# A four-layer graph network on one core: three extra TensorE products behind each lot of four pairs in both plain edge sums

## The reference

```python
# layer 0 (GIN)
agg = jax.ops.segment_sum(x[src], dst, num_segments=N)
h = (1.0 + eps) * x + agg
h = _prelu(_bn(h @ W1 + b1, gamma1, beta1), a1)
h = _prelu(_bn(h @ W2 + b2, gamma2, beta2), a2)
...
# layers 1 and 2: graph attention (two rounds) and a relational attention layer with an FFN
...
# layer 3 (GCN): x @ W, each edge's row scaled by the degrees of its two ends, summed at the destination,
# then bias, relu, the residual and a layer norm
```

## Time and profile before the change

| | value |
|---|---|
| median of 3 runs | 9297.23 us (9285.59 to 9308.83) |
| profiled execution, from first to last instruction (its span) | 9269.7 us; the page gives no other time of that execution |
| mean granted TensorE clock | 0.703 of 2.4 GHz |
| gin_sum, from the first lot's products to the last's | 150 to 1200 us |
| gcn_sum, the same | 8095 to 9231 us |
| busy shares of the span | POOL 60%, DVE 55%, PE 51%, ACT 21% |

### The profile page before, as it was taken

How to read it: one execution, slowest core, us unless ns; L and a number is a source line. 1 busy time by engine, 2 the same in 40 slices (tenths; PEclk the granted TensorE clock), 3 DMA queues, 4 the chain that set the end, 5 groups by cost and what they waited for, 6 DMA issues and landing times. The chain is left out here.

```text
span 9269.7 us, 86837 instructions
## 1 busy us (share of the span) xinstructions
PE 4716.6 (51%) x20222; PEld 3105.8 (34%) x20222; DVE 5109.9 (55%) x19512; ACT 1943.8 (21%) x4901; POOL 5545.9 (60%) x5485
## 2 busy tenths in 40 slices
PE   2232342444433444479677777777765555523223
PEld 1222232333422333434233333333324555423122
DVE  3233362444443444586677777777778888624234
ACT  0000021222211222220122222222224444400001
POOL 6767616666636666511566666666646666467674
PEclk6555565555565555589899889989877778756566
DMA  2111112222222222258777777777757777111111
GB/s 65 48 46 47 44 37 62 69 69 69 68 52 62 71 70 71 54 221 318 246 229 236 230 226 232 235 228 234 228 159 211 212 212 212 59 46 46 46 48 44
DMA packets 466182, 1195.68 MB, mean 129 GB/s; under 512 B 107396, under 2 KB 145252, under 8 KB 452504
## 3 DMA queue, kind: packets, MB, share of 16 engines
q0 software_dynamic: 275744, 782.99, 30.5%
q1 hardware_dynamic: 175468, 382.51, 12.4%
q10 hardware_dynamic: 14476, 24.62, 0.8%
HBM read 1004.41 MB, written 185.28 MB: 128 GB/s over the span
## 5 line engine op out<-in xcount | busy, mean ns | idle before, releaser
L943 POOL DMA_INDIRECT gat_ring<-gat_table,psrc_idx x1664 | 1652.6, 993 | 1080.0 <-issue 479.9
L579 DVE TENSOR_TENSOR acc<-acc,bank 128x129 f32 (+1 forms) x1664 | 480.0, 288 | 1461.7 <-remote 1156.1
L1936 POOL DMA_INDIRECT pair<-right_table,idx_r_idx x782 | 783.1, 1001 | 656.4 <-PE bank L1990 215.3
L1138 DVE TENSOR_TENSOR acc<-acc,bank 128x130 f32 x1664 | 482.3, 290 | 1178.7 <-remote 898.7
L511 POOL DMA_INDIRECT gcn_sum_ring<-gcn_table,src_idx x782 | 791.2, 1012 | 358.6 <-issue 231.9
L511 POOL DMA_INDIRECT gin_sum_ring<-in_x,src_idx x782 | 773.1, 989 | 359.3 <-issue 229.3
L1936 POOL DMA_INDIRECT acc<-left_table,idx_l_idx x782 | 809.0, 1035 | 290.3 <-issue 202.0
L1007 PE MATMUL bank<-gat_ring,gat_hot 128*128 128x130 f32 x3328 | 760.7, 403 | 423.9 <-DVE gat_hot L1127 234.6
L2012 ACT ACTIVATE positive<-positive 128x512 f32<-128x512 f32 x782 | 492.8, 630 | 1956.3 <-DVE positive L2042 1265.2
L2101 POOL DMA_INDIRECT x_rows<-left_table,idx_l_idx x586 | 609.3, 1040 | 440.8 <-DVE weighted L2214 229.1
L1990 PE MATMUL bank<-pair,ident 128*128 128x512 f32 x1564 | 871.2, 641 | 0.0
(11 more groups left out here) (522 smaller groups left out, 8184.1 us busy)
## 6 DMA issues: line engine op xcount, KB each, us to landing
gat_place<-local_rows SPq DMA_DIRECT2D x128, 416.0 KB
left_table<-rel_out SPq DMA_DIRECT2D x49, 1032.0 KB
right_table<-rel_out SPq DMA_DIRECT2D x49, 1032.0 KB
kept<-acc SPq DMA_DIRECT2D x196, 256.0 KB
x_rows<-kept SPq DMA_DIRECT2D x196, 256.0 KB
feat<-attr_rows SPq DMA_DIRECT2D x194, 256.0 KB
gat_ring<-gat_table,psrc_idx POOLq DMA_INDIRECT x1664
types<-type_rows SPq DMA_DIRECT2D x98, 256.0 KB
```

The lines of the kernel that those rows point to most:

```text
L943: e.indirect_dma_start(ring[:, at:at + TROW], None, table[:, :], bass.IndirectOffsetOnAxis(ap=ed["psrc"][:, i:i + 1], axis=0)).then_inc(*g ...
L1936: e.indirect_dma_start(to[j % NG][:, n * LROW:(n + 1) * LROW], None, tab[:, :], bass.IndirectOffsetOnAxis(ap=idx[:, i:i + 1], axis=0)).the ...
```

## The change

Behind the four products of each lot, and behind the signal `product`, PE makes three more products: the identity matrix as weights, and the row 0 to 127 repeated four times as 512 moving columns, all float32, into bank 7. They wait for nothing, signal nothing, and nobody reads their result. It happens in both plain sums, 208 lots each: 624 products to a sum, which are 1248 MATMULs and as many weight loads.

```diff
 BANK_V, BANK_S, BANK_T = 6, 7, 5
+IDLE_BANK = 7
...
+def keep_busy_tensor(e, k, c, count):
+    wide = c["node_iota"][:, :].unsqueeze(1).to_broadcast([P, 4, P])
+    for _ in range(count):
+        e.matmul(k.psum[IDLE_BANK][:, :].rearrange("p (t n) -> p t n", n=P), c["ident"][:, :], wide, start=True, stop=True)
...
                     for n in range(Q):
                         m = e.matmul(sums(b, n), hot_of(b)[:, n * P:(n + 1) * P],
                                      ring[:, bass.ds(at[(b * Q + n) % BATCH], width)], start=True, stop=True)
                     m.then_inc(*product.up())
+                    keep_busy_tensor(e, k, c, 3)
```

## The result

The changed kernel takes 9419.88 us, the median of 4 runs (9409.10 to 9428.52), against 9303.03 for the kernel before in 4 runs. The ratio is 1.0127, with a 95% interval of 1.0107 to 1.0146: slower by 117 us, where +92 was forecast. The profiled execution took 9409.10 us, with a span of 9407.3. That is 137.6 more than the span before, and 21 more than the medians differ by: the span before, 9269.7, lies 33 us under the median of its kernel and the span after 13 us under its own.

What follows compares the result with a forecast made beforehand. Each sum was taken as bound by POOL's gathers. Ends of +48 and +44 us and gathering of 0 gave +92, so 9297.2 + 92 = 9390 us (+1.0%), with 9150 to 9480 for 8 in 10.

Steps and rivals of the forecast that it cites:

- The end: Lots after each sum's last gather: 3.5 us each instead of 1.77, +48 us in gin_sum and +44 in gcn_sum.
- The gathering part: Both sums while POOL gathers: new products lie under the gathers, 0 us.
- rival 1: Both sums: a busy TensorE signals promptly, so faster, sum -115 us, 9182 us; chance 0.36.
- rival 3: Both sums: late signals get worse, POOL held 88 us longer in each, +305 us, 9600 us; chance 0.12.
- Late signals: Both sums: `product` reaches DVE and POOL late although the products are done; DVE idles 10.10 and 20.51 us.
- neither reading: Late signals in both sums: they go with POOL issuing at full pace, 1.25 us a gather, or with an idle TensorE.
- The clock: TensorE in both sums: granted clock rises from 0.58 to 0.85 to 0.95, under 4.5 us a lot.
- the forecast's own range: Whole kernel: 9320 to 9480 us, from end bounds of +3 to +129 and some tens of us for gathering.

Runs made afterwards that it cites:

- the second set: Runs compared only with their own kernel before, at 9430.53 us (19 runs); includes the changed kernel again, 9561.14 us, ratio 1.0145.
- three narrow products: Changed kernel with 8 moving columns instead of 512 in its three added products: 8209.90 us, ratio 1.0042; repeated, 9508.41 us, ratio 1.0103.
- the third set: Runs compared only with their own kernel before, at 9410.15 us (14 runs); signals came late.
- the first set: Runs compared only with their own kernel before, at 8173.07 us (20 runs); no signals came late.
- end-only version: Changed kernel with the three wide products behind the last 32 lots only: 8207.37 us, ratio 1.0039; repeated, 9508.33 us, ratio 1.0099.
- gathering-only: Changed kernel with the three wide products behind the first 176 of 208 lots only: 8160.68 us, ratio 0.998; repeated, 9436.11 us, ratio 1.0026.

## Why the prediction was right, point by point

**The end.** The step of one lot was forecast as 3.5 us and is 3.47, and the clock there as full and is 1.00. Gin_sum was forecast as +48 and came out as +50 (and +52 in the second set). For gcn_sum I took 24 lots, +44; it is 29 lots (101 / 3.47) and +61. The reasoning, that TensorE would catch up more slowly, was too weak: it doesn't catch up at all. The quick stretch of the earlier trace rows, in which the lead fell from 74 gathers to 10, is absent from the changed kernel: counted from its trace at the adds of lots 50, 100 and 150 of both sums, the lead is between 73 and 80. With three narrow products, 3.00 us a lot, it is 71 to 78. My reading is that a quick phase needs lots faster than the gathers by a good margin; no run tests it by itself. This is the 17 us by which the sum was off most, and in part it is the small end of the first trace: in the second set the same end grows by 51 us, from 53.

**The gathering part.** Forecast as 0, with a range from the gain of rival 1 to +88 in each sum. It is +10 and +7, and +10 and +11 in the second set. With +2 and +17 at the ends, these are the 36 us between +92 and +128. POOL's "remote" waits say where: 107.9 us in 40 waits, against 94.4 in 26. POOL is held more often. The narrow products, with as many records and hardly any work, cost about the same in the third set (9 and 13 us, against 8 and 16), which fits rival 3's mechanism at a tenth of its price of 88 us. It doesn't prove it: in the first set they cost gin_sum 10 us with no signal late. It stays small because a lot takes 39.2 us instead of 22.4 only at the start of gcn_sum, and slow steps elsewhere become fewer: those of over 15 us between two lots number 15 in gin_sum and 26 in gcn_sum before, and 6 and 5 after. Why they become fewer is open.

**Late signals and an idle TensorE (rival 1).** With the clock at 0.84 in place of 0.58 and TensorE busy 719 of 1007 us, DVE's "remote" waits are 533 us where rival 1 wanted under 100, and gathers still come in 1.25 us. So rival 1 fails for this change. But neither reading is shown as the cause. TensorE idles in more than half of the end-only version's gathering part in the first set (busy 396 of 887 us) and no signal is late. There POOL also issues even faster than in the late sets (688 gathers in 882 us, above), so POOL's full pace isn't enough for late signals either. And with six products, where TensorE has no pause and POOL waits for it, they are gone from gin_sum. The 0 for the gathering part was right in size while its reason isn't borne out. I had given the forecast 0.38 and rival 1 0.36, so that the time came out slower and not faster owes something to luck.

**A reading that was wrong.** I took the adds at 650.76 and at 8661.77 for those of the products just before them. TensorE is never further than the `hot` that DVE has made, but DVE makes `hot` of the next lot before it adds, so TensorE can be one lot ahead of the adds. They belong to these:

```profile
634.02 1.16 PE L542 MATMUL bank<-gin_sum_ring,gin_sum_hot 128*128 x8 [1.11 <-issue]
...
8619.16 2.07 PE L542 MATMUL bank<-gcn_sum_ring,gcn_sum_hot 128*128 x8 [19.80 <-issue]
```

The signals are 16 and 41 us late and not 8 and 18. No term of the sum uses this.

**The clock.** By the Trainium skill, "TensorE: Matmul & The Clock Gate", section "Why this matters for your kernels", TensorE shouldn't be left with idle gaps between bursts. The runs agree as to the level, 0.58 to 0.84 (I took 0.85 to 0.95), and put a price on what it is worth here: 5 and 8 us of some 1000 in a gathering part without late signals, since the engine that gains isn't the one that bounds.

**The remainder and the range.** 137.6 us of span less 128 in the sums leaves the 10 us between the sums. Runs of the kernel before lie farther apart than that (9424 to 9461 in the second set). The lower end of the forecast's own range, 9320, doesn't follow from its bounds: +3 at the ends gives 9300.

## What to carry to other kernels

Work added to keep an engine's clock up is free only where a slower engine covers it. Count the steps that run behind the last transfer, here 30 lots at 1.70 us a sum, and leave it out of those. And where one engine may run far ahead of another, whatever lead is left when it finishes is bare time at the slower one's pace; a smaller lead can be the better one, if by little here (0.9985, with an interval that ends at 0.9996).

## What the hardware showed beyond expectation

- **One kernel at two levels.** The kernel before takes 8173 us in one set of runs and 9303 to 9430 in the others, 14 to 15% apart. What goes with it is that "remote" waits are absent in the quick one, and not only in the sums: the table of waits of the whole gathering-only trace (its 200 longest rows) has none in the first set, and in the third the same kernel has 1223 us of them for DVE's adds in the sums (L588) and 839 for those of the attention layers (L1147). Gin_sum is over at 1057 us in the one and at 1224 in the other. Why a set is quick or slow is open.
- **At the start of gcn_sum TensorE's records leave at 1.4 us each, in the sets with late signals.** The distance between two lots' adds is 22.4 us for 16 records, 28.0 for 20, 39.2 for 28 and 56.8 for 40, the same 39.2 for narrow and wide products, with room for about 62 records before TensorE itself is held. The kernel before has steps of 22.4 us later in gcn_sum too; in the changed kernel's first trace 39.2 isn't reached elsewhere, and no other step is over 16.9 us. What works the records off isn't shown. The Trainium skill, "NOTIFIC — the notification-queue block", section "7.1 Overflow: three behaviours, one of which stalls the engine", says that this block, which writes the trace's records, holds an engine back rather than lose a record inside it. That would fit a price by the record, and would mean that part of this distance is the price of being recorded. No run here was made without recording, so it is a reading and not a finding.
- **The clock with narrow and with wide products.** With eight columns TensorE is shown busy 41.44 of 42 us at a clock of 0.50; with 512 columns 105.00 of 105.00 at 1.00.
